# A first layer's weight preparation in single, tabulated steps, with part of its sums on VectorE

## The reference

```python
def _L0_ffn_ref(x, Wg, routing_bias, W1, W2, W3, Ws1, Ws2, Ws3):    # E, K = 8, 4; H = 341
    gate = einsum('bsd,ed->bse', x, Wg) + routing_bias
    _, top_idx = top_k(gate, K)
    weights = softmax(where(mask > 0, gate, -inf)) * mask           # mask: the 4 chosen of 8
    out = _swiglu(x, Ws1, Ws2, Ws3)                                 # the shared expert
    h1, h2 = einsum('bsd,ehd->ebsh', x, W1), einsum('bsd,ehd->ebsh', x, W2)
    eo = einsum('ebsh,edh->ebsd', sigmoid(h1) * h1 * h2, W3)
    return out + einsum('ebsd,bse->bsd', eo, weights)
x = x + 0.5 * ffn(layernorm(x))
x = x + attention(layernorm(x))      # 16 heads of 64, causal, W_qkv and W_out
x = x + 0.5 * ffn(layernorm(x))
```

## Time and profile before

| | us |
|---|---|
| median of 3 runs | 739.27 (738.42 to 740.68) |
| the profiled execution | 738.95 |
| its span | 737.2 |
| PE busy | 673.0 (91%) |
| DVE busy | 640.2 (87%) |
| ACT busy | 580.9 (79%) |
| POOL busy | 483.0 (66%) |

### The profile page before, as it was taken

The page is one execution under the profiler, slowest core; times in us unless marked ns, Lnnn a source line. Parts: engine busy times, 40 slices in busy tenths (PEclk is TensorE's granted clock), DMA queues, the critical chain, the costliest instruction groups (busy, mean ns, idle before and its releaser), DMA issues.

```text
span 737.2 us, 20502 instructions
## 1 busy us (share of the span) xinstructions
PE 673.0 (91%) x7601; PEld 447.1 (61%) x7601; DVE 640.2 (87%) x1728; ACT 580.9 (79%) x1155; POOL 483.0 (66%) x563
## 2 busy tenths in 40 slices
PE   2687979998899899899999799999999998999997
PEld 1365655565566666566666456665656765666665
DVE  1678998999999899899889999989999977889886
ACT  5787955697899888799888799889799993565553
POOL 3124655476788857688866679886588984555554
PEclk9988999998999999999999999999999999999999
DMA  7700000056589725578835579872479873000000
GB/s 207 221 1 1 2 1 1 2 80 104 92 134 141 129 44 98 98 128 137 132 74 83 91 116 131 136 124 44 88 131 144 145 121 54 16 2 1 15 3 15
DMA packets 216967, 60.58 MB, mean 82 GB/s; under 512 B 203682, under 2 KB 216100, under 8 KB 216868
## 3 DMA queue, kind: packets, MB, share of 16 engines
q1 hardware_dynamic: 216868, 59.28, 46.9%
HBM read 7.87 MB, written 1.05 MB: 12 GB/s over the span
## 4 chain that ended last, share of the span: by engine, by line
PE 37%; DVE 27%; ACT 18%; issue 9%; DMA 4%; POOL 4%; SPq 1%; DVEq 0%; ACTq 0%; POOLq 0%
PE bank L857 11%; PE bank L859 11%; PE bank L858 11%; ACT probs L1119 5%; DVE glu L1280 5%; DVE glu L1284 4%; DVE probs L1355 4%; DMA pT<-paired 3%; DVE xs L1298 3%; ACT glu L1095 3%; PE bank L980 3%; ACT gluh L1102 2%; POOL paired L830 1%; ACT xn L1061 1%; POOL glul L826 1%
## 5 line engine op out<-in xcount | busy, mean ns | idle before, releaser
L826 POOL TENSOR_TENSOR glul<-glu,gluh 128x512 f16<-128x512 f32 x192 | 222.4, 1160 | 125.5 <-ACT gluh L1102 124.9
L830 POOL TENSOR_TENSOR paired<-probs,paired 128x512 f16<-128x512 f32 x160 | 186.2, 1164 | 32.6 <-ACT paired L1127 31.3
L1095 ACT ACTIVATE glu<-bank,tanh_scale 128x512 f32<-128x512 f32 x192 | 130.8, 681 | 87.1 <-PE bank L859 86.0
L857 PE MATMUL bank<-w3h,gluh 128*128 128x128 f16 x960 | 174.2, 222 | 3.7 <-DVE xs L1298 2.4
L859 PE MATMUL bank<-w3h,glul 128*128 128x128 f16 x960 | 174.1, 222 | 0.0
L858 PE MATMUL bank<-w3l,gluh 128*128 128x128 f16 x960 | 174.1, 222 | 0.0
L1280 DVE SCALAR_TENSOR_TENSOR glu<-glu,bank 128x512 f32<-128x512 f32 x192 | 131.0, 682 | 36.6 <-ACT glu L1095 35.6
L1284 DVE SCALAR_TENSOR_TENSOR glu<-glu,bank 128x512 f32<-128x512 f32 x192 | 132.1, 688 | 20.5
L1119 ACT ACTIVATE probs<-probs,exp_bias 128x128 f32<-128x128 f32 (+3 forms) x256 | 131.7, 551 | 8.2 <-POOL exp_bias L838 8.1
L1355 DVE CUSTOM_DVE_ANT_0 probs<-bank,causal,score_scale 128x128 f32<-128x128 f32 (+3 forms) x256 | 127.9, 546 | 3.6 <-POOL paired L830 2.7
L1102 ACT ACTIVATE gluh<-glu 128x512 f16<-128x512 f32 x192 | 119.1, 621 | 12.1 <-DVE glu L1284 12.1
(11 more groups left out here) (189 smaller groups left out, 1488.2 us busy)
## 6 DMA issues: line engine op xcount, KB each, us to landing
pT<-paired SPq DMA_TRANSPOSE x160, 3.2
attention_raw<-in_L_attn_W_qkv SPq DMA_DIRECT2D x6, 256.0 KB, 5.7
xs<-in_L_attn_inputs SPq DMA_DIRECT2D x4, 256.0 KB, 5.1
out<-xs SPq DMA_DIRECT2D x4, 256.0 KB, 2.9
vh<-in_L_ffn_W SPq DMA_DIRECT2D x6, 128.0 KB
pT<-in_L_ffn_W SPq DMA_DIRECT2D x6, 128.0 KB
raw_more<-in_L_ffn_W SPq DMA_DIRECT2D x4, 128.0 KB
attention_raw<-in_L_attn_W_out SPq DMA_DIRECT2D x2, 256.0 KB, 6.9
```

What stands on the lines that cost most here:

```text
L826: pool.tensor_tensor(glul[pair][:, :], g[:, :], gluh[pair][:, :], ALU.subtract).then_inc(glu_low)
L830: pool.tensor_tensor(paired[n % PAIRED][:, 1, :], probs[n % PROBS][:, :], paired[n % PAIRED][:, 0, :], ALU.subtract).then_inc(probs_low)
L857: pe.matmul(ps, high, mhigh, start=first, stop=False)
L1095: act.activation(g[:, :], psum[b1.bank][:, :], ACT.Tanh, scale=tanh_scale[:, j:j + 1]).then_inc(tanh_made)
```

## The change

The preparation of layer 0 is cut into single steps, and a table says at which tile each is issued. In the table a letter and an expert make a step: m measures, g gathers a group, s spreads it (with `scale_units`), t, u and v transpose the first, second and third matrix into a bank that stays held, p, q and r take its high and low part and free the bank. There are four groups instead of three, the first two experts being one. `ADDED_BY` says who measures an expert: VectorE (V) for experts 0, 1, 3, 5 and 6, in three reductions each, ScalarE (A) for the others. A tile's `hidden` waits for the first two matrices alone, and `down` for the third. The float32 copy of the layer norm is a step of its own (`norm_copy`), issued one call later; the bank is held until then, and VectorE's low part no longer waits for the copy. Ranks are made in three instructions instead of five operations: a difference table, one comparison with a table that holds 0 or minus the least normal number, one reduction. The router's steps in layer 0 start two tiles earlier, those of the attention weights two steps later.

```diff
-GROUPS = [[0, 1, 2], [3, 4, 5], [6, 7, 8]]
+GROUPS = [[0, 1], [2, 3], [4, 5], [6, 7, 8]]
+
+ADDED_BY = "VVAVAVVAA"
...
-PREPARE_AHEAD = 3
...
+PREPARE = {-3: "m0 u0", -2: "m1", -1: "g0 v0 s0 t0", 0: "p0 q0 r0 m2", 1: "t1 p1 u1 q1 m3", 2: "g1", 3: "v1 r1",
+           4: "t2 s1 p2 u2 q2", 5: "v2", 6: "r2 m4 t3 m5 p3 u3 q3", 7: "v3 r3", 8: "g2", 9: "t5 v4 s2",
...
+ROUTE_STEP = 4
...
-ATTENTION_MEASURES = 5
+ATTENTION_MEASURES = 7
...
+    def hold_filled(self, readers=1):
+        use = self.hold(readers)
+        self.fills[use.bank] += 1
+        return use
...
+        self.add("load_expert", n=n, left=self.raw_left.get(n - RAWS), added=self.measured.get(n - RAWS))
+
+    def measure_expert(self, n):
+        by = ADDED_BY[n]
+        self.added[by] += 1
+        self.measured[n] = by, self.added[by]
+        self.add("measure", n=n, by=by, k=self.added[by])
+
+    def gather(self, g):
+
+        assert all(n in self.measured for n in GROUPS[g])
+        self.add("gather_max", g=g, added=dict(self.added), use=self.bank())
+
+    def spread(self, g):
+        self.add("spread_max", g=g, use=self.bank())
+        self.add("scale_units", g=g)
+
+    def turn_weights(self, n, k):
+        use = self.hold_filled()
+        turned = self.turned.setdefault(n, {})
+        turned[k] = use
+        self.add("turn_weights", n=n, k=k, use=use)
+        if len(turned) == 3:
+            self.raw_left[n] = use
+            if n + RAWS < NE:
+                self.load_expert(n + RAWS)
+
+    def prepare_weights(self, n, k):
+        use = self.turned[n][k]
+        self.add("prepare", n=n, k=k, s=self.split(use))
+        self.release(use)
+        self.weights_ready[n, k] = use
+
+    def prepare(self, i):
+        for stage, n in map(tuple, PREPARE.get(i, "").split()):
+            n = int(n)
+            if stage in "tuv":
+                self.turn_weights(n, "tuv".index(stage))
+            elif stage in "pqr":
+                self.prepare_weights(n, "pqr".index(stage))
+            elif stage == "m":
+                self.measure_expert(n)
+            elif stage == "g":
+                self.gather(n)
+            else:
+                self.spread(n)
...
+        s = self.split(self.hold_filled(2) if halves < 2 else self.bank())
+        self.add("norm_turn", i=i, s=s, halves=halves, left=self.halves_left[halves])
         self.xn_left = s.use
-        self.halves_ready[halves] = s.use
+        self.halves_ready[halves] = s.use._replace(d=1)
+        if halves < 2:
+            yield
+            self.add("norm_copy", use=s.use, gate_left=self.gate_left)
+            self.release(s.use)
...
-                self.prepare_ahead(i)
+                self.prepare(i)
...
-                self.measure_ahead(MEASURES[i][0], MEASURES[i][1])
-                while self.measured <= MEASURES[i][2]:
-                    self.measure_expert()
...
         next(norm)
+        self.prepare(-3)
         next(norm)
-        self.measure_expert()
+        self.prepare(-2)
         next(norm, None)
-        self.measure_expert()
-        self.measure_expert()
+        self.prepare(-1)
...
+        def raw_free(q, s):
+            if s["left"]:
+                q.wait_ge(filled[s["left"].bank], s["left"].f + 1)
+                by, count = s["added"]
+                q.wait_ge(measured[by], count)
...
-                    q.wait_ge(measured, GROUPS[g][-1] + 1)
+                    for by, count in s["added"].items():
+                        if count:
+                            q.wait_ge(measured[by], count)
...
+                    drain_of(s["w_ready"])
...
-                    if s["halves"] < 2:
-                        if s["gate_left"]:
-                            q.wait_ge(filled[s["gate_left"].bank], s["gate_left"].f + 1)
-                        act.activation(xnT32[:, :], psum[use.bank][:, :], ACT.Copy).then_inc(gate_x)
+                elif kind == "norm_copy":
+                    use = s["use"]
+                    q.wait_ge(drained[use.bank], use.n + 1)
+                    if s["gate_left"]:
+                        q.wait_ge(filled[s["gate_left"].bank], s["gate_left"].f + 1)
+                    act.activation(xnT32[:, :], psum[use.bank][:, :], ACT.Copy).then_inc(drained[use.bank])
...
+                elif kind == "measure" and s["by"] == "V":
+                    n = s["n"]
+                    g = group_of(n)
+                    i, left, kinds, at = n % RAWS, HID - 2 * P, len(GROUPS[g]), GROUPS[g].index(n)
+                    sums = greatest[g][:, :].rearrange("p (k n) -> p k n", n=kinds)[:, :, at]
+                    q.wait_ge(consts_made, consts)
+                    q.wait_ge(raw_in[i], raw_loaded(n))
+                    q.wait_ge(padded, pads[n])
+                    v.tensor_reduce(sums[:, 0:2], raw12[i][:, :, 0:2, :], AX.XY, ALU.add, apply_absolute_value=True)
+                    v.tensor_reduce(sums[0:left, 2:4], raw12[i][0:left, :, 2, :], AX.X, ALU.add,
+                                    apply_absolute_value=True)
+                    v.tensor_reduce(sums[:, 4:5], raw3[i][:, 0:len(TILES_OF[n]) * P], AX.X, ALU.add,
+                                    apply_absolute_value=True).then_inc(measured["V"])
...
-                    v.tensor_tensor(beats, rows_j, rows_i, ALU.is_gt)
-                    chained(v.tensor_tensor(ties, rows_j, rows_i, ALU.is_equal))
+                    chained(v.tensor_tensor(ahead_by, rows_j, rows_i, ALU.subtract))
...
-                    chained(v.tensor_tensor(ties, ties, earlier[:, :, :].unsqueeze(1).broadcast_to([P, NT, E, E]),
-                                            ALU.mult))
+                    chained(v.tensor_tensor(ahead_by, ahead_by, earlier[:, :, :].unsqueeze(1).broadcast_to([P, NT, E, E]),
+                                            ALU.is_gt))
                     chain()
-                    chained(v.tensor_tensor(beats, beats, ties, ALU.add))
-                    chain()
-                    chained(v.tensor_reduce(rank[:, :, :], beats, AX.X, ALU.add))
+                    chained(v.tensor_reduce(rank[:, :, :], ahead_by, AX.X, ALU.add))
```

More of the change, by code:

```diff
@@ L18 @@
 TOP_K = 4
+LEAST = 2.0 ** -126
 MASKED = -8e37
@@ L123, in __init__ @@
         self.drains, self.fills = [0] * BANKS, [0] * BANKS
-        self.splits = self.norms = self.tiles = self.parts = self.gates = 0
+        self.splits = self.norms = self.tiles = self.parts = 0
         self.glu_taken = 0
@@ L167, in load_expert @@
     def load_expert(self, n):
-        self.add("load_expert", n=n, left=self.raw_left.get(n - RAWS))
-    def measure_group(self, stage):
-        g = self.stages[stage]
-        self.stages[stage] += 1
-        self.add("spread_max" if stage else "gather_max", g=g, use=self.bank())
-    def measure_expert(self):
-        self.add("measure", n=self.measured)
-        self.measured += 1
-    def prepare_expert(self):
-        n = self.prepared
-        self.prepared += 1
-        s = [self.split(use) for use in (self.bank(), self.bank(), self.bank())]
-        self.add("prepare", n=n, s=s)
-        self.raw_left[n] = s[2].use
-        self.expert_ready[n] = [k.use for k in s]
-        if n + RAWS < NE:
-            self.load_expert(n + RAWS)
@@ L190, in prepare_ahead @@
-    def prepare_ahead(self, i):
-        last = min(i + min(PREPARE_AHEAD, i), HT - 1)
-        while self.prepared < NE and TILES_OF[self.prepared][0] <= last:
-            g = next(g for g, of in enumerate(GROUPS) if self.prepared in of)
-            self.measure_ahead(g, g)
-            self.prepare_expert()
-            if self.prepared - 1 == GROUPS[g][0]:
-                self.add("scale_units", g=g)
-    def measure_ahead(self, gathered, spread):
-        while self.stages[0] <= gathered:
-            while self.measured <= GROUPS[self.stages[0]][-1]:
-                self.measure_expert()
-            self.measure_group(0)
-        while self.stages[1] <= spread:
-            self.measure_group(1)
+        self.add("load_expert", n=n, left=self.raw_left.get(n - RAWS), added=self.measured.get(n - RAWS))
@@ L265, in down @@
         self.parts += 1
-        self.add("down", part=PARTS.index((j, n)), k=t["k"], pair=t["pair"], first=first, last=last, use=use)
+        self.add("down", part=PARTS.index((j, n)), k=t["k"], pair=t["pair"], first=first, last=last, use=use,
+                 w_ready=self.weights_ready[n, 2])
         done = self.parts
@@ L834, in gpsimd @@
                     for use in s["uses"]:
-                        q.wait_ge(drained[use.bank], use.n + 1)
+                        q.wait_ge(drained[use.bank], use.n + use.d)
                     q.wait_ge(masks_made, masks)
@@ L1030, in scalar @@
                     q.wait_ge(scales_made, group_of(n) + 1)
-                    for k, high in enumerate((w1h, w2h)):
-                        split = s["s"][k]
-                        high_of(split, psum[split.use.bank][:, 0:HID], high[:, units_of(n)], scale_of(n, k))
-                    split = s["s"][2]
```

(12 more changed lines are left out.)

100 lines of the change are left out of this document (43 added, 57 removed), and 2 rows, old and new, of the table PREPARE.

## The result

The changed kernel took 728.95 us (median of 4, 727.43 to 731.38) against 739.61 for the kernel before (median of 4, 738.42 to 740.68): a ratio of 0.9859, 95% interval 0.9825 to 0.9894. It is 10.7 us faster; 731.6 was forecast, and the range held. So the two profiles are only 7.6 us apart.

A forecast was written before the change was run, and what follows sets the result against it. Layer 0 was held by PE waiting for ScalarE's sums, with VectorE the bound once that gap goes; 5.6 + 1.5 + 1.3 - 0.8 = 7.6 us off 738.95, plus 0.3 for the median, gave 731.6 us, range 725.5 to 737.5.

The forecast's parts named there:

- The start: Start of layer 0: first hidden product at 15.7 us instead of 20.46, a gain of 4.7 us.
- The gap: Layer 0, second group: tile 5's hidden product at 31.9 us instead of 41.95; 8 us gained at equal VectorE work.
- The rest of layer 0: Layer 0 behind the gap: VectorE is the bound and gives part of the 8 us back, leaving 5.6 at layer 1.
- What layer 0's lead is worth: From layer 1 to the end: the 5.6 us gained at layer 1 was counted in full in the final time.
- Behind layer 0: Layers after layer 0: removed rank operations give 1.5 us just behind it and 1.3 in the six layers further on.
- The held bank: Layer norm's bank kept 12 us longer, until the copy: PE has seven banks instead of eight, 0.8 us lost.
- fourth rival: Layers beside attention: the held bank binds and slows PE by a fifth, 13 us lost, 744 us; chance 0.06.
- The first: Layer 0: VectorE gives back nearly all, 2.5 us won, 736.7 us; chance 0.17 together with the fifth.
- the fifth: Start: VectorE's sums wait for a load or pads, 4.7 us goes, 736 us; chance 0.17 together with the first.
- The second: PE, not VectorE, is the bound: layer 0 is 10 us shorter, layers behind give 3, 726 us; chance 0.17.
- The third: Layer 0: PE paced in small pieces, its granted clock drops to 0.73, 738 us; chance 0.05.
- the term of layer 0: Layer 0's share of the summed gain: 5.6 us, with 1.7 and 10 as ends.

The follow-up runs named there:

- e1: The changed kernel with its table kept but all nine experts' sums on ScalarE: 729.8 us, ratio to the kernel before 0.9862.
- e6: The changed kernel with VectorE's sums of experts 3, 5 and 6 made twice, results unused: 730.4 us, ratio to the kernel before 0.9877.
- e2: The changed kernel with the old groups and order of preparation and all sums on ScalarE, new ranks kept: 731.19 us, ratio to the kernel before 0.9874.
- e0: The changed kernel run again without edits, in another set: 729.14 us, ratio to the kernel before 0.9851.
- e13: The changed kernel with old preparation order, all sums on ScalarE and old ranks: 734.88 us, ratio to the kernel before 0.9939.
- e9: The changed kernel with the old five-operation ranks put back, all else kept: 732.52 us, ratio to the kernel before 0.9895.
- e4: The kernel before with the new three-instruction ranks alone: 732.52 us, ratio to the kernel before 0.9885.

## Why the prediction was right, and where it was not

**The start: right.** Forecast 15.7 for the first hidden product, measured 15.85. The reductions were forecast at 0.69, 0.42 and 0.55 us and took 0.69, 0.41 and 0.54. Expert 1's sums start at 9.81 us, where they were forecast at 8.8 (the wait before them is for its load); the steps behind them were so much shorter.

**The gap: right, a little too small.** Tile 5's hidden product was forecast at 31.9 and came at 30.14. The cause, PE waiting for ScalarE's sums, was right as read: those waits are gone. But it was the order of the steps more than the engine: with the table and all sums on ScalarE tile 5 comes at 32.67 (e1).

**The rest of layer 0: the time right, the reason half.** Layer 1 was forecast at 95 to 97 and came at 94.59. VectorE at over 95% was forecast for the stage behind; it was 94.5% for 20 us, then 88 and 82%, with PE at half its clock from 68 to 72. e6 gives the size: a microsecond of VectorE's work cost 0.4 us of the layer, where the sum had charged all of it.

**What layer 0's lead is worth: the step that failed.** The sum let 5.6 us at layer 1 stand to the end. The layer's 6.9 us were there. But undoing the whole preparation (e2) cost 2.1 us by the medians against e0, 1.1 to 1.7 by the ratios, with intervals that overlap; with the old ranks (e13 against e9) it cost 2.4, or 3.3 by the ratios, and those intervals do not meet. Most of the lead was lost later, in the profiles in layer 5, where PE waited longer for `pT`. One execution of each shows this, and runs of the changed kernel alone lie 4 us apart (727.43 and 731.38).

**Behind layer 0: mis-sized.** The ranks were put at 1.5 in layer 0, 1.5 just behind and 1.3 further on, with 0 to 4 as ends for the last. They were worth 7.9 us by themselves (e4) and 3.4 on top of the rest (e9 to e0). In e4's profile nothing of it is in layer 0, 1.1 us is left of layer 1, and 5.0 come further on. The step priced most removed operations at 0.42 us and VectorE's share of the chain, and did not count that a long one holds the gated product up and PE behind that.

**The held bank and what came with it: wrong in sign as a whole.** The bank was charged 0.8 us, the copy out of the low part's way was put at nothing, and the router's later place had no term. The kernel with these three and the third weight's own wait (e13) won 5.5. What the bank alone costs, no run shows: the new wait of 1.9 us for `xnT` is one for the later copy, not for a bank, and PE's waits of over 0.6 us for banks behind layer 0 did not grow (7.3 us in all, 11.0 before). So the fourth rival falls.

**The rivals.** The first (VectorE gives back nearly all) and the fifth (the start no earlier) fall by the traces. The second (PE bound, more won) named 726: more was won, though through the ranks and the router's place. The third (the clock) was there twice for some 4 us, behind idle stretches, and did not decide: layer 0's mean was 0.93 (15.85 to 94.59), where it had been 0.92. The sum of 7.6 us equals the difference of the two profiled executions, 738.95 - 731.38, by luck: the term of layer 0 was too large for the end and those of the ranks and of the router's place too small, and the two executions are not typical; by the medians the gain was 10.7 to 10.9 us.

**Open:** why `pT` comes later in layer 5 when the layers ahead are quicker, and how the 5.5 us of e13 split between the copy, the router's place and the wait of the third weight.

## What to carry to other kernels

A lead won in the first layer is worth only what the later layers do not take up: test it by putting the old order back, not by the time at which the next layer starts, and look at the start of every later layer for where it goes. Beside a busy GpSimd, count VectorE's operations by their SBUF inputs and not by their length: sixteen spare ones with two cost 6.8 us more than sixteen with one, and leaving one operand in PSUM was worth as much as the rearranged preparation or more. Where two edits remove waiting of the same kind, measure each alone and both together before giving either its share.

## What the runs showed of the hardware

- A reduction with absolute value took 0.69 us for 512 columns in two dimensions, 0.41 for 256 and 0.54 for 384; one of 256 columns without it took 0.42.
- Operations on VectorE with two SBUF inputs ran from 0.42 up to 1.4 us; each of the long ones began while a GpSimd instruction ran, and all but one of those with 256 columns ended 0.28 to 0.29 us behind it. With one of the operands in a PSUM bank the same operation took 423 to 426 ns in all of eight.
- Sixteen such operations, of 0.42 us each when undisturbed, cost 8.2 to 9.0 us of the end; sixteen reductions of the same length 1.5 to 2.8 us by the same measures, not clear of noise.
- PE was busy 0.91 of 4 us and then had a granted clock of 0.61 for 4 us; it was busy 1.38 of 4 us and then had 0.50 for 4 us, 0.80 for the next 4, and 1.00 behind that.
